# Attention with whole value groups and spread transposes; FFN with a third step of lag, and the bias added by VectorE

## The reference

```python
q, k, v = ((x @ W.T).reshape(N, S, 16, 32).transpose(0, 2, 1, 3) for W in (Wq, Wk, Wv))
attn = softmax(einsum('nhqd,nhkd->nhqk', q, k) / sqrt(32), axis=3)
x = layernorm(x + einsum('nhql,nhld->nhqd', attn, v).transpose(0, 2, 1, 3).reshape(N, S, 512))
w = (weights >= 0) * 2.0 - 1.0
y = clip(einsum('bsi,oi->bso', x, w) * scale + bias, -100, 100)
out = layernorm(x + y)
```

## Time and profile before

| | |
|---|---|
| profiled execution | 2738.42 us, of which the span of instructions is 2736.6 us |
| TensorE busy | 98% of the span, 38720 matmuls |
| ScalarE busy | 83% |
| VectorE busy | 81% |
| GpSimd busy | 22% |
| granted TensorE clock | 0.993 of full speed, mean |

### The profile page before, as it was taken

How to read it: one execution, slowest core, us unless ns; L and a number is a source line. 1 busy time by engine, 2 the same in 40 slices (tenths; PEclk the granted TensorE clock), 3 DMA queues, 4 the chain that set the end, 5 groups by cost and what they waited for, 6 DMA issues and landing times. The chain is left out here.

```text
span 2736.6 us, 92216 instructions
## 1 busy us (share of the span) xinstructions
PE 2690.3 (98%) x38720; PEld 1722.2 (63%) x38720; DVE 2214.1 (81%) x2687; ACT 2277.5 (83%) x2726; POOL 613.0 (22%) x663
## 2 busy tenths in 40 slices
PE   9999999999999999999999999999999999996998
PEld 7888888755555555555555555555555555555776
DVE  7443333489999999989999999998999999986887
ACT  5333333399999999999999999999999999984665
POOL 1000000022222222222222222222222222224665
PEclk9999999999999999999999999999999999998999
DMA  6555555589898999989899998989999898976664
GB/s 232 193 194 185 184 186 193 192 173 194 173 200 175 197 181 194 194 167 204 172 202 183 187 198 167 209 170 200 185 180 201 173 204 170 190 144 189 208 209 135
DMA packets 311610, 512.33 MB, mean 187 GB/s; under 512 B 20930, under 2 KB 201154, under 8 KB 309060
## 3 DMA queue, kind: packets, MB, share of 16 engines
q0 software_dynamic: 73440, 267.42, 52.7%
q1 hardware_dynamic: 228004, 221.56, 26.1%
q10 hardware_dynamic: 9792, 17.83, 1.8%
HBM read 121.90 MB, written 117.44 MB: 87 GB/s over the span
## 5 line engine op out<-in xcount | busy, mean ns | idle before, releaser
L812 ACT ACTIVATE probs<-banks 128x1024 f32<-128x1024 f32 x2048 | 1896.7, 1073 | 11.7 <-PE banks L642 5.4
L642 PE MATMUL banks<-score_rows 97*32 97x512 f16 x16384 | 1269.6, 380 | 4.0 <-issue 3.9
L674 PE MATMUL banks<-probs,v_keys 128*32 128x256 f32 x16384 | 1268.4, 379 | 0.0
L674 PEld LDWEIGHTS banks<-probs,v_keys 128*32 128x32 f32 x16384 | 539.6, 110 | 377.7 <-issue 0.9
L614 POOL DMA_DIRECT2D total<-partial x510 | 440.1, 863 | 1465.6 <-DVE partial L902 675.7
L902 DVE TENSOR_TENSOR partial<-partial,probs 128x1024 f32<-128x1024 f32 x640 | 749.4, 1213 | 0.0
L642 PEld LDWEIGHTS banks<-score_rows 97*32 97x32 f16 x16384 | 463.2, 96 | 344.5 <-ACT probs L812 17.4
L898 DVE TENSOR_TENSOR partial<-probs 128x1024 f32<-128x1024 f32 x512 | 603.5, 1220 | 67.8 <-issue 55.8
L356 DVE TENSOR_TENSOR qk_lo<-banks,qk_hi 128x512 f16<-128x512 f32 x128 | 88.4, 690 | 241.2 <-ACT qk_hi L311 241.1
L311 ACT ACTIVATE qk_hi<-banks 128x512 f16<-128x512 f32 x128 | 76.0, 594 | 184.7 <-PE banks L228 184.7
L228 PE MATMUL banks<-xT_hi,w_hi 128*128 128x512 f32 x512 | 197.3, 389 | 0.0
(11 more groups left out here) (95 smaller groups left out, 2220.3 us busy)
## 6 DMA issues: line engine op xcount, KB each, us to landing
total<-partial POOLq DMA_DIRECT2D x510, 512.0 KB, 6.0
scratch_q_raw<-qk_raw SPq DMA_DIRECT2D x16, 1024.0 KB, 5.7
scratch_k_raw<-qk_raw SPq DMA_DIRECT2D x16, 1024.0 KB, 5.7
scratch_v<-v_out SPq DMA_DIRECT2D x16, 1024.0 KB, 5.2
score_rows<-scratch_q_hi SPq DMA_DIRECT2D x128, 128.0 KB, 5.3
score_rows<-scratch_k_hi SPq DMA_DIRECT2D x128, 128.0 KB, 5.5
v_keys<-scratch_v SPq DMA_DIRECT2D x64, 256.0 KB, 7.1
scratch_attn<-wf_scaled SPq DMA_DIRECT2D x64, 256.0 KB, 5.4
```

The lines of the kernel that those rows point to most:

```text
L642: last = nc.tensor.matmul(scores_of(phase, unit)[part, i, :], k_rows[:, h, keys], q_rows[:, h, qb * BLK:(qb + 1) * BLK], start=True, stop= ...
L674: last = nc.tensor.matmul(banks[rows, out_bank(qb), cols], v_keys[:, kt, rows], probs[:, kt % P_RING, h, cols], start=(kt == 0 and part == ...
L812: nc.scalar.activation(probs[:, kt % P_RING, heads, :], scores_of(it % SLOTS, qb * UNITS + u), ACT.Exp, scale=SCALE / GAIN ** 2).then_inc( ...
```

## The change

In `attend`, the two half groups of values become one group of four matmuls with 512 columns, issued behind both pairs of scores. The four transposes of the output are spread over tiles 3, 4, 5 and 6, one after each, with a semaphore increment for each. The pieces of the denominators follow tiles 9 to 12, their transpose tile 14. VectorE's copies follow (after tiles 2, 7 and 13; the inversion stays after 14). After the last block all these are issued in a row, as before.

In `normalise_and_ffn`, y is turned at lag 3, and FFN, CLIP and LN2 move to lags 5, 6 and 7. The bias matmul goes. A DMA spreads the bias over 128 partitions once (256 KB, on SyncE's queue behind the first load of x), and VectorE adds it while it reads the product from PSUM into `biased`; behind the statistics VectorE clips `biased` in SBUF into `clipped`. TensorE waits for `biased` where it waited for the clip.

```diff
-DEN_TILES = (8, 9, 10, 11)
-TURN_TILE = 4
-DEN_TURN_TILE = 13
-OUT_AFTER, TURNED_AFTER, DEN_AFTER, INVERT_AFTER, NORMAL_AFTER = 2, 5, 12, 14, 15
+DEN_TILES = (9, 10, 11, 12)
+TURN_TILES = (3, 4, 5, 6)
+DEN_TURN_TILE = 14
+OUT_AFTER, TURNED_AFTER, DEN_AFTER, INVERT_AFTER, NORMAL_AFTER = 2, 7, 13, 14, 15
...
-        def values(it, qb, kt, part):
+        def values(it, qb, kt):
...
-                last = nc.tensor.matmul(banks[rows, out_bank(qb), cols], v_keys[:, kt, rows], probs[:, kt % P_RING, h, cols],
-                                        start=(kt == 0 and part == 0), stop=(kt == KT - 1), skip_group_check=True)
+                last = nc.tensor.matmul(banks[rows, out_bank(qb), :], v_keys[:, kt, rows], probs[:, kt % P_RING, h, :],
+                                        start=(kt == 0), stop=(kt == KT - 1))
...
+        def turn_output(it, qb, c):
+            if c == 0:
+                pe.wait_ge(a_out, it * QB + qb + 1)
+            cols = slice(c * P, (c + 1) * P)
+            nc.tensor.transpose(banks[:, out_bank(qb), cols], out_sb[:, cols], ident2[:]).then_inc(a_turn, 1)
...
-            if kt == TURN_TILE:
-                turn_output(it, qb)
+            if kt in TURN_TILES:
+                turn_output(it, qb, TURN_TILES.index(kt))
...
-                for half in range(2):
-                    if kt + LAG < KT:
-                        scores(it, phase, qb, kt + LAG, (half,))
...
-                    values(it, qb, kt, half)
+                if kt + LAG < KT:
+                    scores(it, phase, qb, kt + LAG)
...
+                values(it, qb, kt)
...
-    ATTN, LN1, TRANS, FFN, CLIP, LN2 = 0, 1, 2, 4, 5, 6
+    ATTN, LN1, TRANS, FFN, CLIP, LN2 = 0, 1, 3, 5, 6, 7
...
+        sp.dma_start(bias_b[:], bias.partition_broadcast(P)).then_inc(f_bias, 16)
...
-                pe.wait_ge(f_clip, t + 1)
-                nc.tensor.matmul(ffn_bank(s), bias_ones[:], bias_rows[:], start=True, stop=False)
+                pe.wait_ge(f_biased, t + 1)
...
                 dve.wait_ge(f_ffn, t + 1 + 4)
-                dve.wait_ge(f_res[1], t + 1 - 2 + Y_SLOTS)
-                nc.vector.tensor_scalar(clipped[:, s % 2], ffn_bank(s), -MAX_VAL, MAX_VAL, ALU.max, ALU.min).then_inc(f_clip, 1)
+                dve.wait_ge(f_clip, t + 1)
+                nc.vector.tensor_tensor(biased[:, s % 2], ffn_bank(s), bias_b[:], ALU.add).then_inc(f_biased, 1)
             for t, s, which in norms:
                 statistics(t, s, which, (res1, res2)[which], (2 * TPB, Y_SLOTS)[which])
+            t, s = tile(r, j, CLIP)
+            if t is not None:
+                dve.wait_ge(f_biased, t + 1 + 2)
+                dve.wait_ge(f_res[1], t + 1 - 2 + Y_SLOTS)
+                nc.vector.tensor_scalar(clipped[:, s % 2], biased[:, s % 2], -MAX_VAL, MAX_VAL, ALU.max, ALU.min).then_inc(f_clip, 1)
```

More of the change, by code:

```diff
@@ L626, in _, with fast_scores @@
         pe.sem_inc(a_den, 2 * len(DEN_TILES))
-        def fast_scores(it, phase, qb, kt, halves=(0, 1)):
-            if kt == 0 and halves[0] == 0:
+        def fast_scores(it, phase, qb, kt):
+            if kt == 0:
                 pe.wait_ge(a_q[qb], it * FIRST_Q + FIRST_Q)
-            if qb == 0 and kt % TPB == 0 and halves[0] == 0:
+            if qb == 0 and kt % TPB == 0:
                 pe.wait_ge(a_k[kt // TPB], it * FIRST_K + FIRST_K)
-            for half in halves:
+            for half in range(2):
                 unit = qb * UNITS + 2 * kt + half
@@ L644, in fast_scores, with exact_scores @@
                 last.then_inc(a_score, 1)
-        def exact_scores(it, phase, qb, kt, halves=(0, 1)):
+        def exact_scores(it, phase, qb, kt):
             st = it * QB + qb
-            if kt == 0 and halves[0] == 0:
+            if kt == 0:
                 pe.wait_ge(m_q, st * 32 + 32)
-            if kt % TPB == 0 and halves[0] == 0:
+            if kt % TPB == 0:
                 pe.wait_ge(m_k[kt // TPB % 2], (st * QB // 2 + kt // TPB // 2) * 16 + 16)
             keys = slice(kt % (2 * TPB) * P, (kt % (2 * TPB) + 1) * P)
-            for half in halves:
+            for half in range(2):
                 unit = qb * UNITS + 2 * kt + half
@@ L660, in exact_scores @@
                 last.then_inc(a_score, 1)
-        def values(it, qb, kt, part):
+        def values(it, qb, kt):
             st = it * QB + qb
[L665 to L671, removed]
+            if qb == 0 and kt % TPB == 0:
+                pe.wait_ge(a_v[kt // TPB], it * 16 + 16)
+            pe.wait_ge(a_prob, st * UNITS + 2 * kt + 2 + SLOTS)
+            if kt == 0:
+                pe.wait_ge(a_dout, st + 1)
             for h in range(G):
                 rows = slice(HD * h, HD * h + HD)
-                last = nc.tensor.matmul(banks[rows, out_bank(qb), cols], v_keys[:, kt, rows], probs[:, kt % P_RING, h, cols],
-                                        start=(kt == 0 and part == 0), stop=(kt == KT - 1), skip_group_check=True)
[L676 to L686, removed]
+                last = nc.tensor.matmul(banks[rows, out_bank(qb), :], v_keys[:, kt, rows], probs[:, kt % P_RING, h, :],
+                                        start=(kt == 0), stop=(kt == KT - 1))
+            last.then_inc(a_pv, 1)
+        def turn_output(it, qb, c):
[3 more added lines that the diff above has]
+            nc.tensor.transpose(banks[:, out_bank(qb), cols], out_sb[:, cols], ident2[:]).then_inc(a_turn, 1)
         def denominators(it, qb, piece):
@@ L748, in item @@
             else:
-                turn_output(it, QB - 1)
+                for c in range(TPB):
+                    turn_output(it, QB - 1, c)
                 for piece in range(TPB):
@@ L911, in _, with normalise_and_ffn @@
         normalise(ITEMS * QB - 1, 1)
-def normalise_and_ffn(nc, ctx, dram, x, ffn, first, banks, out):
-    wf_hi, wf_lo, bias_ones, bias_rows, _ = ffn
+def normalise_and_ffn(nc, ctx, dram, x, bias, ffn, first, banks, out):
+    wf_hi, wf_lo, _, _, _ = ffn
     def sb(name, shape, dt):
@@ L958, in normalise_and_ffn @@
     f_ffn = sem("f_ffn")
+    f_bias = sem("f_bias")
+    f_biased = sem("f_biased")
     f_clip = sem("f_clip")
@@ L1062, in step @@
                     for part, w in ((yT_hi, wf_hi), (yT_lo, wf_hi), (yT_hi, wf_lo)):
-                        last = nc.tensor.matmul(ffn_bank(s), part[:, s % 4, cols], w[:, c, :], start=False,
+                        last = nc.tensor.matmul(ffn_bank(s), part[:, s % 4, cols], w[:, c, :], start=(c == 0 and part is yT_hi and w is wf_hi),
                                                 stop=(c == DC - 1 and w is wf_lo))
@@ L1117, in _ @@
         dve.sem_inc(f_clip, 2)
+        dve.sem_inc(f_biased, 2)
+        dve.wait_ge(f_bias, 16)
         for which in range(2):
@@ L1224, in build @@
         with ExitStack() as ctx:
-            normalise_and_ffn(nc, ctx, dram, x_blocks, ffn, first, banks, out_tiles)
+            normalise_and_ffn(nc, ctx, dram, x_blocks, bias, ffn, first, banks, out_tiles)
 def layout(inputs):
```

16 lines of the change are left out of this document (9 added, 7 removed).

## The result

| | before | changed |
|---|---|---|
| median | 2738.56 us (2737.49 to 2740.33, 4 runs) | 2800.05 us (2799.55 to 2800.56, 4 runs) |
| ratio, 95% interval | | 1.0224 [1.0206, 1.0242] |
| profiled execution, span | 2738.42, 2736.6 | 2799.84, 2798.0 |

The forecast was 2814 us, of a range of 2776 to 2838. It was 14 us too high. The granted clock is 0.993 in both.

What follows compares the result with a forecast made beforehand. TensorE was taken to bound attention, and a ring through GpSimd the changed last stage. 2738.42 + 50 (spread transposes) + 26 (last stage: +27 for the ring, -1 for start, end and DMA) = 2814 us, range 2776 to 2838.

Steps and rivals of the forecast that it cites:

- TensorE sets attention: Attention: TensorE's row sums to 29.7 us, the whole block, so each thing added is paid in full, 63 times.
- Spread transposes: Attention: four separate transposes each pay entry and exit, +0.80 us a block, +50 us; bounds 0 to +62.
- Rival 1: Attention: a run's price belongs to its semaphore wait, so spreading adds nothing; 2764 us in all, 9%.
- Grouping of the values: Attention: a group costs by columns, so fewer, wider value matmuls save 0; at most 0.16 us a block either way.
- Denominators' transpose: Attention: this single transpose, now after tile 14, was read at 0.41 us; no change in its cost was counted.
- The score slots just fit: Attention: paired score groups leave ScalarE behind by 0.4 to 0.5 us against 0.5 of slack; 0 taken.
- the new wait for the output: Attention: VectorE's output copy must end before TensorE's turn after tile 3; the wait stays hidden by 0.3 us.
- a ring of 4.25 us: Last stage: clip, GpSimd's two additions and the next statistics chain to 4.25 us a step, +0.47, +27 us.
- The signs: Whole kernel: blocks of 30.5 us, single transposes +0.37, ScalarE waiting for scores, steps of 4.25, TensorE idle 0.8 a step.
- One sign of being wrong: Last stage: the forecast would be wrong if GpSimd still waited over 1 us a step.
- Rival 2: Last stage: VectorE alone, not the ring through GpSimd, sets steps of 4.00 us; 2800 us in all, 10%.
- Rival 4: Attention: transposes' weights load under longer value passes, entry and exit vanish, -35 us; 2729 in all, 3%.

Runs made afterwards that it cites:

- e4: Changed attention but with values in half groups as before, transposes still spread over tiles 3 to 6; last stage as before: 2783.92 us, ratio 1.0167.
- e6: Changed attention with every transpose written as four 32-column matmuls by the identity, last stage as before: 2730.95 us, ratio 0.9971.
- e8: Kernel before with only the last stage's lags changed; bias matmul and clip out of PSUM stay: 2726.47 us, ratio 0.9957.
- e5: e3 with each tile's values issued as two half groups of 256 columns, one right behind the other: 2738.22 us, ratio 0.9999.
- e3: Kernel before with whole groups of values behind both score groups, the four transposes in one run after tile 4: 2735.15 us, ratio 0.9989.
- e7: Attention as before, changed last stage with GpSimd's two additions in the other order: 2743.73 us, ratio 1.0018.
- e9: e11 plus the denominators' transpose as four 32-column matmuls and the third lag of e8: 2708.12 us, ratio 0.989.
- e11: Changed attention with the four transposes back in one run behind tile 3's values, last stage as before: 2727.17 us, ratio 0.996.

## Why the prediction was right, point by point

- **TensorE sets attention, and what is added to its row is paid in full.** Right. The block grew by the sum of its pieces, and ScalarE got waits where it had next to none.
- **Spread transposes, +0.80 a block.** Right in mechanism and near in size: 4 x 0.37 - 0.70 is 0.78 with the measured values, and spread alone 46 us (e4). The terms as I wrote them, 1.50 + 0.04 - 0.70, give 0.84 and not 0.80, so the sum should have read 53 us and 2817, and the miss would be 17. The measured 0.37 holds the slower first group already. I also called the 0.26 from a lone transpose to the scores an exit price; 0.11 of it is the turning itself. Rival 1 fell twice: the transposes without a wait cost as much as the one with it, and e6 took the price away with the waits left in. The rule on tiling modes (the Trainium skill, "TensorEngine Tiling (Array Packing)", Key Properties) spoke for this side. By the trace a change of shape costs and a change of instruction within the full array doesn't (e6, e8), which agrees with it; that TensorE drains meanwhile no run here shows.
- **Grouping of the values, 0.** This term failed, and it is most of the miss. It was worth 0.008 to 0.009 us a tile, 0.14 a block, 9 us; 0.16 a block was my bound. I had argued from half the columns in half the time that nothing is fixed. These starts are given to 0.01 us, and a constant of 2.5 ns for each of two passes in a row is under that. The Trainium skill, "TensorE: Matmul & The Clock Gate", Back-to-back issue gap, had about 2.5 ns a matmul; e5 against e3 shows just that for each recorded pass, so the rule I set aside was the better guide. The 3 ns of e5 against before, which I attribute to fewer changes between scores and values, was in no term.
- **Denominators' transpose, 0.** It fell from 0.41 to 0.37, 0.045 a block, 3 us. It starts 0.11 behind the end of the values' turn instead of 0.15. That isn't the whole groups' doing: in e4, with half groups, it starts 0.11 late too, and in e3, where it stands after tile 13 as before, as well. Why it was dearer before stays open. Together: +0.78 - 0.14 - 0.045 = +0.59 a block; 63 times that is 37 us, where I had 50.
- **The score slots just fit, 0; the new wait for the output stays hidden.** Right for this kernel. The copy ends 0.4 before the turn; I had 0.3. The slack was as thin as worked out: with seven tiles between the two transposes (e3) TensorE is held by 0.11 a block.
- **Last stage, a ring of 4.25 us.** Right in size and mechanism: 4.254, and without one of its links 3.93 (e7). The clip in SBUF took 0.41, the end that I chose. The 63 intervals grew by 26.2 us where I had 27; start and end of the stage together gave back 1.5, not 1: +24.8 against +26.
- **The signs.** Blocks, the single transposes, ScalarE's waits, the steps and the releaser of the statistics came as listed. TensorE is idle 0.6 a step by its busy time, not 0.8. One sign of being wrong came too, GpSimd waiting over 1 us a step: it waits 1.73 to 1.80 for the clip. That sign was badly chosen, and doesn't count against the ring: GpSimd is busy for 2.5 of the 4.25 in it, so the forecast itself had it wait 1.7 while VectorE does the statistics and the clip.
- **The total** is 14 us off: 13 in attention and 1 in the last stage, all on the same side; only the slip of 3 us in the sum worked the other way.
- **Rival 2, VectorE alone at 4.00**, is near the measured total (2800), but not by its mechanism: its step of 3.93 needs the other order on GpSimd. A total near a rival's is no evidence for it; the steps are.
- **Rival 4**, entry and exit vanishing, didn't come: the lone visit costs 0.37, far above the 0.14 from which this rival decides. In e6 entry and exit are gone for another reason, the shape, and there the attention is faster than before.

## What to carry to other kernels

On a TensorE that is full, keep work of one array shape together: a lone visit in another shape costs mostly its entry and exit, so run such visits together or write them in the shape around them. Before an engine takes over another's work, look at whether its row has room, and at who waits for what now stands behind what; a clip moved behind the statistics closed a ring through GpSimd that cost more than the instruction itself (0.47 a step against 0.15 in e7). When 1024 tiles repeat, a constant of a few nanoseconds is a term: times read to 0.01 us can't rule it out, so take starts many tiles apart and divide.

## What the runs showed of the hardware

- A lone 128x128 float32 transpose between 32-column matmuls takes 0.37 us of TensorE's row, four in a run 0.70, and the same turn as four 32-column matmuls side by side 0.217 (e6, e9, e11). So one turn alone is cheaper in 32 columns, and four at once should be cheaper on the full array (0.70 against 4 x 0.217 = 0.87, which no run has in a row).
- Between matmuls that use the full array too, four transposes cost 0.11 each and nothing on entry or exit (e8).
- Float32 value matmuls of 256 instead of 512 columns make a tile 5 ns longer (1.730 against 1.725), 2.5 ns for each recorded pass more in a row (e5, e3).
- In a stretch of tiles alone the exponentials of 128x1024 start 0.904 us apart (e3).
- VectorE's two aggregations take 0.24 us when another instruction lies between them and the statistics, 0.42 right behind; the reciprocals, which wait for ScalarE, start no earlier for it (e7).
- In e6 the tiles between the two turns are some 2 ns longer than in e9 (medians of 1.727 against 1.7255 from values to values, though the shortest are 1.725 in both). What makes this difference stays open.
